# The values product moved ahead of the next scores in a fused attention and mixture-of-experts kernel

## The reference

```
xn = layernorm(x)
latent = xn @ w_kv_down; k, v = split(latent @ w_kv_up); q = xn @ w_q      # 16 heads of 64
att = softmax(where(causal, q k^T / 8, -inf)); attn = (att v) @ w_out
moe = for 8 experts: y_e = down(silu(gate xn) * up xn), top 2 of sigmoid(xn gate_w^T + lb_bias),
      an expert's rows are weighted by the mean weight over the rows that it got
shared = the same network with 256 hidden columns, for all rows
out = x + attn + moe + shared
```

## Time and profile before

| | |
|---|---|
| median of 3 runs | 1014.62 us (1012.88 to 1015.33) |
| span of the profiled execution | 995.0 us |
| own time of the profiled execution | not listed; the median lies 19.6 us above the span |
| PE busy | 955.2 us (96%) |
| DVE, ACT, POOL busy | 707.6 (71%), 651.3 (65%), 339.3 us (34%) |
| chain that ended last | PE 84%, "issue" 7%, DVE 6% |
| DMA | 142.77 MB, 143 GB/s |

### The profile page before, as it was taken

How to read it: one execution, slowest core, us unless ns; L and a number is a source line. 1 busy time by engine, 2 the same in 40 slices (tenths; PEclk the granted TensorE clock), 3 DMA queues, 4 the chain that set the end, 5 groups by cost and what they waited for, 6 DMA issues and landing times.

```text
span 995.0 us, 20239 instructions
## 1 busy us (share of the span) xinstructions
PE 955.2 (96%) x7200; PEld 768.4 (77%) x7200; DVE 707.6 (71%) x2016; ACT 651.3 (65%) x1801; POOL 339.3 (34%) x333
## 2 busy tenths in 40 slices
PE   5689998899999999999999999999999999999998
PEld 4456776787888888888888887888878778777776
DVE  5779699896666657666666756666576786888884
ACT  3747666665767666676667766677756775677771
POOL 0331113223233243443344433435131444444441
PEclk9799999999999999999999999999999999999999
DMA  6487424542225425465253552546433542533321
GB/s 194 163 308 244 162 102 146 164 169 82 100 81 181 144 96 171 119 201 181 86 181 118 183 187 92 151 154 181 160 101 126 165 129 73 180 108 105 124 86 43
DMA packets 66003, 142.77 MB, mean 143 GB/s; under 512 B 7856, under 2 KB 40880, under 8 KB 64112
## 3 DMA queue, kind: packets, MB, share of 16 engines
q1 hardware_dynamic: 52896, 91.77, 27.9%
q0 software_dynamic: 12432, 49.29, 15.9%
q10 hardware_dynamic: 576, 0.42, 0.1%
HBM read 104.76 MB, written 36.70 MB: 142 GB/s over the span
## 4 chain that ended last, share of the span: by engine, by line
PE 84%; issue 7%; DVE 6%; POOL 2%; DMA 1%; ACT 1%; DVEq 0%; POOLq 0%; SPq 0%
PE PS L670 15%; PE PS L671 14%; PE PS L672 14%; PE PS L712 13%; PE PS L703 13%; PE PS L693 12%; PE PS L819 2%; PE PS L811 1%; DVE pp L1245 1%; DVE acc L985 1%; DMA xs<-xs_scratch 1%; PE PS L718 1%; POOL rstd L1350 1%; DVE ohA L1196 1%; DVE acc L1158 0%
## 5 line engine op out<-in xcount | busy, mean ns | idle before, releaser
L924 ACT ACTIVATE pp<-pp,nmax 128x128 f32<-128x128 f32 (+3 forms) x512 | 280.7, 550 | 100.7 <-DVE nmax L1245 100.7
L1245 DVE CUSTOM_DVE_ANT_0 pp<-PS,maskw 128x128 f32<-128x128 f32 (+3 forms) x512 | 215.1, 483 | 4.7 <-PE PS L693 3.4
L1401 POOL TENSOR_TENSOR yy<-yf,yy 128x512 fp32r<-128x512 f32 x63 | 82.0, 1302 | 287.4 <-ACT yy L860 286.9
L703 PE MATMUL PS<-ident,pp 128*128 128x128 f32 x1280 | 165.1, 275 | 1.6 <-DVE acc L1215 1.5
L693 PE MATMUL PS<-qk 64*128 64x256 f32 (+2 forms) x1536 | 145.6, 335 | 15.9 <-issue 8.4
L703 PEld LDWEIGHTS PS<-ident,pp 128*128 128x128 f32 x1280 | 141.2, 141 | 16.7 <-issue 9.6
L712 PE MATMUL PS<-pt,vv 128*64 128x512 f32 (+3 forms) x1024 | 152.0, 439 | 0.0
L693 PEld LDWEIGHTS PS<-qk 64*128 64x128 f32 x1536 | 113.5, 189 | 31.4 <-issue 17.6
L712 PEld LDWEIGHTS PS<-pt,vv 128*64 128x64 f32 x1024 | 67.8, 136 | 90.4 <-issue 74.1
L860 ACT ACTIVATE pt<-PS 128x384 f32<-128x384 f32 (+1 forms) x215 | 108.5, 512 | 3.3 <-PE PS L703 3.2
L1251 DVE COPY pt<-PS 128x384 f32<-128x384 f32 x169 | 99.1, 591 | 12.8 <-PE PS L703 12.8
(11 more groups left out here) (169 smaller groups left out, 2072.1 us busy)
## 6 DMA issues: line engine op xcount, KB each, us to landing
rb<-rr_scratch SPq DMA_DIRECT2D x128, 128.0 KB
wr<-wm_scratch SPq DMA_DIRECT2D x16, 768.0 KB, 5.8
y_scratch<-acc SPq DMA_DIRECT2D x39, 256.0 KB
acc<-in_x SPq DMA_DIRECT2D x15, 512.0 KB, 5.9
wm_scratch<-hh SPq DMA_DIRECT2D x10, 768.0 KB, 4.0
xs_scratch<-wr SPq DMA_DIRECT2D x7, 1024.0 KB, 5.4
xs<-xs_scratch SPq DMA_DIRECT2D x7, 1024.0 KB, 4.8
xn_scratch<-acc SPq DMA_DIRECT2D x8, 512.0 KB, 3.4
```

Of the source, the lines that this page charges most:

```text
L703: done = e.transpose(o, pp[:, i % 4, P_AT[t] + 128 * kt:P_AT[t] + 128 * kt + 128], ident[:, :])
L924: e.activation(scores, scores, ACT.Exp, scale=-1.0, bias=nmax[:, b, t:t + 1], accum_out=rs[:, i % 4, 2 * t + h:2 * t + h + 1]).then_inc(a_ ...
L1245: e.tensor_tensor_reduce(pp[:, b, P_AT[t]:P_AT[t] + n], g[:, at:at + n], maskw[:, 512 - n:512], -1.0, 3e38, ALU.add, ALU.min, accum_out=nm ...
L1401: e.tensor_tensor(yy[:, i % 2, 1, :], yf[:, :], f32(yy[:, i % 2, 0, :]), ALU.subtract).then_inc(g_yl, 1)
```

## The change

A step now begins with `recip`, two ticks, and attend P-1; the scores of pair P+1 follow at once, then the fill due at 4P and the transposes. Before, attend stood behind the scores and that fill. The same pieces are done by the same engines.

```diff
--- before.py
+++ after.py
@@ -193,14 +193,15 @@
         if P == NHT // 2 - 1:
             put("recip_rows", P)
             tick()
+        if 1 <= P <= NHT // 2:
+            tick(2)
+            put("attend", P - 1)
+            tick(1 if P < NHT // 2 else 8)
         if following:
             for j in range(3):
                 put("scores", P + 1, j)
                 tick()
         place(4 * P, end)
-        if 1 <= P <= NHT // 2:
-            put("attend", P - 1)
-            tick(1 if P < NHT // 2 else 8)
         for h in range(2):
             if this:
                 for j in range(3):
```

## The result

| | before | changed |
|---|---|---|
| median, first measurement | 1014.98 us (4 runs) | 1096.37 us (1094.17 to 1098.94, 4 runs) |
| median, measured again | 996.32 us (13 runs) | 1095.13 us (1094.74 to 1097.47, 4 runs) |
| span of the profiled execution | 995.0 us | 1092.4 us |
| PE busy | 955.2 us (96%) | 1001.1 us (92%) |
| DVE, ACT, POOL busy | 707.6, 651.3, 339.3 us | 697.9, 629.6, 337.5 us |

The ratio is 1.081 (95% interval 1.0785 to 1.0835) in the first measurement and 1.100 (1.0981 to 1.1018) in the second. The forecast was 1039 us, 1013 to 1056. In the first measurement and in the first four experiments (e1 to e4) the kernel before took 1015 us, in all others 996 to 997 us, and each ratio is to the runs of before of its own set. The profiled execution of before, with its 995.0 us, is like the second kind, and so is a new profile of it (994.9 us).

The account below looks back on a forecast made before the run. From 250 us on PE's matmuls bound the kernel; in late steps the new loop through `rb` would. -5.5 + 1 + 18 + 3 + 1 + 3 + 4 = +24.5 us on 1014.6 gave 1039 us, range 1013 to 1056.

Parts of the forecast that it names:

- The parts that I had put on `rb`: Waiting for the `rb` load: +18 us in late steps, +3 for late loads landing behind larger transfers, +3 between 250 and 780 us.
- wrong in size: Sign set beforehand: late steps of 12 or 15 us, instead of about 13, would show the size to be wrong.
- the 19.6 us: Distance of the runs' median above the profiled span of 995.0 us, taken as unchanged: base 1014.6 us.
- The waits that attend meets: Attend right behind the previous step's transposes waits for their copies: 0.25 us in each of ten steps, +1 us counted.
- The loop that closes: Each step, y, `yy`, exponentials, `rrT` and the `rb` load back to y: 12.96 us against 11.31, +18 us late.
- wrong in the mechanism: Sign set beforehand: PE's new waits lie on copies of transposes or on banks while `rb` has long landed.
- Yy's copy, which in the new order also stands before the exponentials: Link on ACT between y and the exponentials, priced at 0.54 us until the next instruction.
- Between 250 and 780 only a late load matters: Steps of 14 to 17 us there exceed 12.96, so only late `rb` loads cost: +3 us.
- my turn: One round per step from y through ACT and the DMA of `rb` to the next y: 12.96 us, between 12.6 and 15.8.
- The start: Up to 250 us: DVE waits for the first `rb` load, routing packs into fewer steps; +4 us, bounds -3 and +12.
- The joints: Array shape changes on PE, three per step instead of four, 0.09 us each over 62 steps: -5.5 us.
- Rival C: Loop binds with `rb` landing 5 us after the second issue: turn 14.5, 38 us late, 10 middle; 1053 to 1070, chance 0.13.

Follow-up runs that it names:

- e1: Changed kernel with ACT's copy `yy` moved behind the exponentials (lag 7 ticks instead of 3), first set: 1089.86 us, ratio 1.0706.
- e4: Kernel before with only the two empty ticks added at the begin of each step, nothing moved, first set: 1020.04 us, ratio 1.0043.
- c5: Changed kernel without the wait for `rb` (multiply by ones, division by row sums left out in all pairs but the last), later set: 1073.88 us, ratio 1.0776.
- c4: Changed kernel with ACT's copy `yy` moved behind the exponentials (lag 7 ticks instead of 3), later set: 1069.96 us, ratio 1.0727.
- e10: Changed kernel with the copy `yy` made on GpSimd instead of ACT: 1045.61 us, ratio 1.0511.
- e12: Changed kernel with `yy` copied by GpSimd and no wait for `rb` (division by the row sums left out): 1028.27 us, ratio 1.0324.
- c3: Changed kernel with `yy` behind the exponentials and no wait for `rb` (division left out but in the last pair), later set: 1049.19 us, ratio 1.0531.
- e5: Changed kernel with attend one place later, behind the first of the three scores pieces: 1029.76 us, ratio 1.0332.
- e6: Kernel before with the two empty ticks and the fill moved behind attend, all three scores pieces staying ahead of it: 1011.17 us, ratio 1.0137.
- e3: Changed kernel with `yy` behind the exponentials and no wait for `rb` (division left out but in the last pair), first set: 1077.05 us, ratio 1.0599.
- e2: Changed kernel without the wait for `rb` (multiply by ones, division by row sums left out in all pairs but the last), first set: 1075.93 us, ratio 1.0579.

## Why the prediction was wrong

**Right:** the direction, that PE had no slack after 250 us, that the new order closes a loop once a step, one of its links, and the price of a joint. The load of `rb` was put at 4.05 us from its first issue; in the step shown it was 3.65 (SP issued it at 1002.81, y began at 1006.46), in the late steps of this trace that wait for it 3.4 to 3.9:

```profile
1002.81 1.11 SPq L605 DMA_DIRECT2D rb<-rr_scratch  x2
```

The parts that I had put on `rb` (18 and 3 late, 3 in the middle) make 24 us; taking the wait away gave 21 (c5). But they lie elsewhere: 5 early, 9 in the middle, 7 late. I had 21 of them late, so that the totals agree is luck. The steps of about 13 us that I named as the mark were 14.2 and 13.9, toward the 15 that the prediction called "wrong in size". And the base of the sum was off: the 19.6 us are no distance between span and time, which is 1.8 to 2.1 us in every run of this record; the median of 1014.6 and the span of 995.0 come from the two kinds of runs told above.

**The step that failed is "The waits that attend meets", +1 us,** and with it "The loop that closes", which knew only the way through `rb`. I priced the waits from the mean duration of a copy, at 0.25 us for each of ten attends, as if a copy began when its transposes end. It begins when ACT and DVE come to it, and in the new order they come to it behind `yy`, eight exponentials, `vv` and `k`. The listing of PE's waits in the changed kernel has them:

```profile
PE PS L713 <- DVE pt L1252: 6.4, 12, 1.4
...
PE PS L704 <- ACT pt L861: 3.4, 10, 0.6
```

and they are the smaller part, since a wait inside a group of matmuls shows only as its length (3.48 us for 2.37). Attend waits for the last copy of the round, and the next scores, which start the round again, stand behind attend. Before, the scores were issued 3.7 us ahead of attend (893.42 and 897.14), so the next exponentials could begin while the copies were still being made. The prediction named this very sign for "wrong in the mechanism": PE's new waits lie on copies of transposes (the other half of the sign, `rb` long landed, isn't met). Without either wait and without `yy` 31 us are left (e12): 17 more in the late steps, where the rows show the round, 19 more in the first 18 steps, where I haven't followed it, and some 4 less in the middle and at both ends.

**"Yy's copy, which in the new order also stands before the exponentials"** was seen, but priced at 0.54 us. It has a second wait: in every second pair for the older output product, whose second half is due at 4P + 0.2 and so stands behind the scores. I read the wait for y and overlooked that one. It costs 25 us (c4), and 49 with the copy itself (e10).

**"Between 250 and 780 only a late load matters", +3 us,** measured 25.9. The comparison was of 12.96 us with steps of 14 to 17. But my turn was the one through the DMA alone. Without `yy`'s wait 12 of the 25.9 come back (c4), without `rb`'s 9 (c5), with both 24 (c3): the round with its waits is longer than even these steps. The loads also land later there than I took them, past the 6.85 us of my upper bound. SP and DVE of the changed kernel, 7.3 us from the first issue to y:

```profile
321.00 1.10 SPq L605 DMA_DIRECT2D rb<-rr_scratch  x2
```

```profile
328.30 0.69 DVE L1264 TENSOR_TENSOR yf<-PS,rb 128x512 f32<-128x512 f32 x1 [4.64 <-DMA rb<-rr_scratch]
```

**"The start", +4 us,** measured 32.5. I had bounded it by 12, from one late first load. DVE is busy for 85 of 100 us there before the change, and it carries the last part of the round. e4 puts 5.6 us on the ticks. Of the rest, 15 us go with the two waits (c3), and 10 of 32.5 are still there with one scores piece ahead (e5); that the round is longest where DVE is busiest is argued, not shown.

**The joints, -5.5 us,** can't be told apart in any run's time, since every variant loses more than that. In the starts of matmuls the price holds. Before, attend follows the last fill after 0.32 us (896.82 to 897.14); where transposes follow the same fill, as in e6, it is 0.23. PE before, then in e6:

```profile
896.82 0.40 PE L672 MATMUL PS<-xs,wqL 128*128 128x512 f32 x1
```

```profile
949.34 0.39 PE L674 MATMUL PS<-xs,wqL 128*128 128x512 f32 x1
949.57 1.25 PE L705 MATMUL PS<-ident,pp 128*128 128x128 f32 x10
```

e6 changes shape three times per step, like the changed kernel. Every second of its late steps takes 11.15 to 11.21 us instead of 11.31, and its 28 middle steps are 3.3 us shorter than before. In the changed kernel this gain is swallowed by the waits. The Trainium skill, TensorEngine Tiling (Array Packing), Key Properties, says that changing the tiling mode drains TensorE; these rows agree.

**Rival C** (slow landings, 1053 to 1070) was nearest in size. Its reason doesn't hold in the late steps (3.4 to 3.9 us), where it had put 38 us; in the middle ones some loads do land so late, and all waits for `rb` together are worth 21 us (c5).

## What to carry to other kernels

When a piece is moved on one engine, follow each other engine's queue once round until it comes back to the moved piece, with every wait of every instruction on the way, and add it up. If the way is longer than the step, the step takes its length, however idle each engine is: here the round set the pace while ACT, which carries the longest part of it, was busy 58%. A copy that is wanted at once costs not its duration but its place in the queue. Idle time of an engine on the round is no sign of slack, and where it stands depends only on which instruction heads its queue. ACT stood before the exponentials for 100.7 us in the kernel before and for 6.1 in the changed one, where `yy` heads the queue and takes the waiting; in e12, with the round closed and `yy` gone, it stood there for 214.6 us. The group of e12:

```profile
L926 ACT ACTIVATE pp<-pp,nmax 128x128 f32<-128x128 f32 (+3 forms) x512 | 281.1, 551 | 214.6 <-DVE nmax L1248 214.6
```

What does tell is a small dose of work on that engine in both kernels: the same dose cost 21 us in the closed round and 6.4 us in the open one.

## What the runs showed of the hardware that I had not expected

In the first set TensorE's semaphores came late. Scores whose records begin at 980.22 in e3 were passed to DVE at 984.40; what else this pass waits for is work of two pairs before. In c3, the same kernel, scores of the same pair begin at 962.12 and DVE's first pass stands at 963.14. DVE's row in e3, then in c3:

```profile
984.40 0.29 DVE L1247 CUSTOM_DVE_ANT_0 pp<-PS,maskw 128x128 f32<-128x128 f32 x1 [2.24 <-remote]
```

```profile
963.14 0.29 DVE L1247 CUSTOM_DVE_ANT_0 pp<-PS,maskw 128x128 f32<-128x128 f32 x1 [0.22 <-PE PS L695]
```

The same is seen elsewhere in that set: DVE, idle, begins its first pass more than 1.3 us after the scores' start, where 1.0 is usual, in 4 steps of the changed kernel, 7 of e2, 10 of e1, 13 of e3 and 14 of e4, but in at most two of any later trace. The surplus adds up to 5, 7, 24, 26 and 32 us.

e3 took 28 us more in that set than in the later one, e1 20 us, the kernel before 18 us, the changed kernel 1 us and e2 2 us. For the four with traces of both sets that is within some 5 us of these sums; e4 wasn't run again, and the kernel before has no trace from a run of 1015 us. e3 and c3 ran on the same chip, so it isn't the chip alone. What it was stays open. It made e1 and e3 look nearly worthless, and it was found only by running them, and before, again.
